# Signs written straight into the convolution's lanes, and another order of loads and stores

## What is computed

```python
x = channel_shuffle(x, 2);  xa, xb = split(x, 2, axis=1)
x1 = leaky_relu(gconv3x3(sign(x), w1, groups=2))        # 3x3, 64 -> 32 channels, 2 groups
x2 = batchnorm_train(x1, g1, b1)                        # statistics over all images
x3 = batchnorm_train(concatenate((x2 + xa, xb)), g2, b2)
x3 = channel_shuffle(x3, 2)
x4 = leaky_relu(gconv3x3(sign(x3), w2, groups=2))
x4 = batchnorm_train(x4, g3, b3)
out = concatenate((x4 + x3[:, :32], x3[:, 32:]))
```

## Time and profile before

| | us |
|---|---|
| median of 3 runs | 3279.19 (3274.48 to 3287.09) |
| profiled execution, device time | 3276.55 |
| its span, first to last instruction | 3274.8 |
| PE, PEld, DVE, ACT, POOL busy | 85%, 70%, 65%, 62%, 58% |
| mean granted TensorE clock | 0.943 of full speed |

### The profile page before, as it was taken

How to read it: one execution, slowest core, us unless ns; L and a number is a source line. 1 busy time by engine, 2 the same in 40 slices (tenths; PEclk the granted TensorE clock), 3 DMA queues, 4 the chain that set the end, 5 groups by cost and what they waited for, 6 DMA issues and landing times. The chain is left out here.

```text
span 3274.8 us, 116147 instructions
## 1 busy us (share of the span) xinstructions
PE 2788.1 (85%) x47624; PEld 2283.9 (70%) x47624; DVE 2114.6 (65%) x3114; ACT 2026.7 (62%) x4321; POOL 1900.8 (58%) x1450
## 2 busy tenths in 40 slices
PE   3888837777629999999989999999999999999992
PEld 2555525565428887888878778887888878878882
DVE  3445422222359878797887968778797877969660
ACT  1222112222248887888877877887888877878860
POOL 0000000000148888888887888888888888878870
PEclk9999968888869999999999999999999999999996
DMA  4555368888436766666666666666676666666552
GB/s 105 148 145 143 99 158 208 201 217 209 119 126 189 204 194 194 197 198 191 204 193 189 202 187 188 199 196 201 187 202 193 202 194 184 199 192 194 172 169 69
DMA packets 476972, 586.45 MB, mean 179 GB/s; under 512 B 175768, under 2 KB 420960, under 8 KB 476512
## 3 DMA queue, kind: packets, MB, share of 16 engines
q1 hardware_dynamic: 358240, 488.14, 54.1%
q10 hardware_dynamic: 118272, 91.76, 8.8%
HBM read 351.92 MB, written 201.14 MB: 169 GB/s over the span
## 5 line engine op out<-in xcount | busy, mean ns | idle before, releaser
L1251 PE MATMUL acc_p<-abuf,vbd 128*32 128x102 f32 (+7 forms) x27648 | 1088.2, 333 | 113.8 <-DMA abuf<-weight_scratch 110.4
L1251 PEld LDWEIGHTS acc_p<-abuf,vbd 128*32 128x32 f32 (+1 forms) x27648 | 907.1, 144 | 295.8 <-DMA abuf<-weight_scratch 128.0
L1088 ACT ACTIVATE dwt<-xp,wts 128x224 f32<-128x224 f32 x2016 | 799.7, 482 | 107.0 <-ACT wst L1111 101.7
L164 PE MATMUL cv<-cin,wb 128*64 128x392 bf16 x6912 | 636.3, 348 | 150.1 <-DMA cin<-sg 150.1
L960 DVE TENSOR_TENSOR pr<-mh_p,ht 128x864 f32<-128x864 f32 x672 | 668.9, 1051 | 23.2
L164 PEld LDWEIGHTS cv<-cin,wb 128*64 128x64 bf16 x6912 | 449.7, 115 | 330.6 <-issue 98.9
L1230 PE MATMUL win_p<-pr,smat 128*128 128x160 f32 x4032 | 610.4, 306 | 10.4 <-POOL pr L1046 8.5
L1230 PEld LDWEIGHTS win_p<-pr,smat 128*128 128x128 f32 x4032 | 555.9, 190 | 30.9 <-POOL pr L1046 8.9
L1029 POOL TENSOR_TENSOR dwt<-dwt 128x896 f32<-128x896 f32 x224 | 512.0, 2286 | 4.7 <-ACT dwt L1088 4.7
L1043 POOL TENSOR_TENSOR pr<-pr 128x576 f32<-128x576 f32 x224 | 317.1, 1416 | 283.3 <-DVE pr L960 283.3
L1172 PE MATMUL om_p<-wts,omin 64*64 64x216 f32 x3584 | 378.6, 351 | 2.4 <-issue 2.4
(11 more groups left out here) (137 smaller groups left out, 2820.2 us busy)
## 6 DMA issues: line engine op xcount, KB each, us to landing
abuf<-weight_scratch SPq DMA_DIRECT2D x1568, 120.0 KB, 2.6
weight_scratch<-wst ACTq DMA_DIRECT2D x224, 400.0 KB, 3.6
xt<-x SPq DMA_DIRECT2D x128, 392.0 KB, 8.5
rows_scratch<-vsb SPq DMA_DIRECT2D x224, 128.0 KB, 3.2
vbd<-rows_scratch SPq DMA_DIRECT2D x896, 32.0 KB, 2.8
cin<-sg SPq DMA_DIRECT2D x128, 203.0 KB, 3.5
x_scratch<-xt SPq DMA_DIRECT2D x64, 392.0 KB, 5.4
y<-x SPq DMA_DIRECT2D x64, 392.0 KB, 4.0
```

Of the source, the lines that this page charges most:

```text
L164: mm = pe.matmul(cv[c][64 * h:64 * h + 64, 0:CN], wb[:, layer, j, k, :], cin[:, u, r:r + CR, k % 3:k % 3 + W], start=(k == 0 and j == 0), ...
L1088: ins = act.activation(dwt[:, j % 2, k, :].rearrange("p (r w) -> p r w", w=W), image[:, r:r + BR, k % 3:k % 3 + W], ACT.Identity, scale=dw ...
L1251: mm = pe.matmul(acc_p[32 * (2 * s + b):32 * (2 * s + b) + 32, 0:TN].rearrange("p (k w) -> p k w", w=W)[:, k0:k1 + 1, x0:x1], vbd[0:K, 1 - ...
```

## The change

ScalarE signs 64 lanes at a time and writes them at once into `cin`, in the lanes that the convolution reads: four instructions of 64x1568 for two of 128x1568. `sg`, `move_signs` and the semaphores `signs_in`, `signs2` are gone; TensorE waits for the signs' own semaphore. The border columns are zeroed in `cin`.

In the first block SP issues x of pairs 0 and 1 right behind the first layer's weights; the second layer's weights are loaded and split in the next block, behind VectorE's statistics of pair 0. At the end of the first pass SP also issues `lin` of pairs 0 and 1 and x of pairs 1 and 0 for the second pass. In the second pass's loop the loads of `lin` (p + 2) and x (p + 3) stand ahead of the stores of x3 (p + 1) and of the result (p). VectorE gets a wait for x of its own.

```diff
-        sg = sb("sg", [128, 2, 2, HH, PW], bf16)
...
-        def move_signs(eng, u, done):
-            for t in range(2):
-                for h in range(2):
-                    eng.dma_start(cin[64 * t:64 * t + 64, u, 1 + HH * h:1 + HH * (h + 1), :],
-                                  sg[64 * h:64 * h + 64, u, t, :, :]).then_inc(done, 16)
+        def write_signs(act, p, u, t, bias):
+            for h in range(2):
+                lanes = slice(64 * h, 64 * h + 64)
+                a = act.activation(cin[64 * t:64 * t + 64, u, 1 + HH * h:1 + HH * (h + 1), 1:1 + W],
+                                   rows(xt[lanes, buf(p), t, :].rearrange("p a f -> p (a f)")),
+                                   ACT.Sign, bias=gs[lanes, u, 3, t:t + 1] if bias else 0.0)
+            return a
+        def split_weights(dve, layer, loads, start):
+            then = steps(dve, w_split, start)
+            dve.wait_ge(w_in, 16 * loads)
+            then(dve.tensor_copy(wb[:, layer, 0], wf[:, :, :]))
...
                         sp.dma_start(wf[at:at + CO, :, oc:oc + 16], w1t[:, :, 16 * t:16 * t + 16]).then_inc(w_in, 16)
+                load_x(sp, 0, x_in[0])
+                load_x(sp, 1, x_in[1])
+                sp.wait_ge(par_in, 32)
...
                 channel_stats(0, 0, 0)
                 group_stats(0, 0)
+                dve.memset(wf[:, :, :], 0.0).then_inc(w_zero, 1)
+                split_weights(dve, 1, 12, 5)
...
-                step(pairs - 4, 0, False)
+                step(pairs - 4, 0)
                 sp.wait_ge(used_ok, pairs - 3)
                 load_x(sp, pairs - 1, x_in[1])
-                step(pairs - 3, 1, False)
-                step(pairs - 2, 0, False)
-                step(pairs - 1, 1, True)
+                for u in range(2):
+                    sp.wait_ge(l1_out[u], 16)
+                    sp.dma_start(lin[:, u, :], l1_d[u, :, :]).then_inc(l1_in[u], 16)
+                step(pairs - 3, 1)
+                sp.wait_ge(used_ok, pairs - 2)
+                load_x(sp, 1, x_in2[1])
+                step(pairs - 2, 0)
+                step(pairs - 1, 1)
+                sp.wait_ge(used_ok, pairs)
+                load_x(sp, 0, x_in2[0])
...
                 def step(p, i, u, last):
-                    pe.wait_ge(signs_in[u], NS * i + NS)
+                    pe.wait_ge(sign_ok, p + 1)
...
                 with sp.Fori(0, pairs // 2 - 2) as i:
                     for u in range(2):
-                        step(2 * i + u, u, False)
                         load_l1(2 * i + u + 2, u)
                         settle(sp)
                         sp.wait_ge(x3_out[u], NX * i + NX)
                         load_x(sp, 2 * i + u + 3, x_in2[1 - u])
+                        step(2 * i + u, u, False)
...
+                    dve.wait_ge(x_in2[u], NX * i + NX)
```

More of the change, by code:

```diff
@@ L171, in evacuate, with steps @@
             act.activation(lt[:, u, CN * c:CN * (c + 1)], cv[c][:, 0:CN], ACT.Copy).then_inc(done, 1)
-        def steps(eng, done):
-            n = [0]
+        def steps(eng, done, start=0):
+            n = [start]
             def then(ins):
@@ L194, in _, with step @@
                         sp.dma_start(wf[at:at + CO, :, oc:oc + 16], w1t[:, :, 16 * t:16 * t + 16]).then_inc(w_in, 16)
+                load_x(sp, 0, x_in[0])
+                load_x(sp, 1, x_in[1])
+                sp.wait_ge(par_in, 32)
+            @block.gpsimd
+            def _(pool):
+                for col in (0, PW - 1):
+                    pool.memset(cin[:, :, 1:1 + H, col:col + 1], 0.0)
+                for row in (0, H + 1):
+                    pool.memset(cin[:, :, row, :], 0.0)
+                pool.memset(eps[:, :], EPS)
+                pool.memset(half[:, :], -0.5).then_inc(cleared, 1)
+                pool.wait_ge(cleared, 1)
+            @block.vector
+            def _(dve):
+                dve.memset(wf[:, :, :], 0.0).then_inc(w_zero, 1)
+                split_weights(dve, 0, 4, 0)
+        x_in2 = [sem("x_again0"), sem("x_again1")]
+        l1_in = [sem("l1_in0"), sem("l1_in1")]
+        l1_out = [sem("l1_out0"), sem("l1_out1")]
+        bx_ok, mv_ok, sq_ok, rhs_ok, grp_ok, neg_ok, m2_ok, var_ok, eps_ok, rstd_ok, sign_ok = map(sem, (
+            "bx_ok", "mv_ok", "sq_ok", "rhs_ok", "grp_ok", "neg_ok", "m2_ok", "var_ok", "eps_ok", "rstd_ok", "sign_ok"))
+        conv_ok, evac_ok, leaky_ok, cross_ok, used_ok = map(sem, ("conv_ok", "evac_ok", "leaky_ok", "cross_ok", "used_ok"))
+        with nc.Block() as block:
+            @block.sync
+            def _(sp):
+                def step(p, u):
+                    sp.wait_ge(leaky_ok, p + 1)
+                    sp.dma_start(l1_d[p, :, :], lt[:, u, :]).then_inc(l1_out[u], 16)
                 sp.wait_ge(w_zero, 2)
@@ L202, in _ @@
                                          w2t[t, :, :, 16 * q:16 * q + 16]).then_inc(w_in, 16)
[L203 to L225, removed]
@@ L228, in l0_passes @@
[L228 to L249, removed]
@@ L251, in _ @@
                 sp.wait_ge(x_in[0], NX)
                 load_x(sp, 2, x_in[0])
-                signs(0, 0)
                 with sp.Fori(0, pairs // 2 - 2) as i:
                     for u in range(2):
-                        step(2 * i + u, u, False)
+                        step(2 * i + u, u)
                         settle(sp)
@@ L524, in step @@
                                      lt[64 * h:64 * h + 64, u, :]).then_inc(l2_out[u], 16)
-                for p in range(2):
-                    load_x(sp, p, x_in2[p])
-                    load_l1(p, p)
                 sp.wait_ge(x_in2[0], NX)
                 load_x(sp, 2, x_in2[0])
-                x3_and_signs(0, 0)
+                store_x3(0, 0)
                 with sp.Fori(0, pairs // 2 - 2) as i:
                     for u in range(2):
-                        step(2 * i + u, u, False)
                         load_l1(2 * i + u + 2, u)
@@ L542, in _ @@
                 load_x(sp, pairs - 1, x_in2[1])
+                step(pairs - 4, 0, False)
+                load_l1(pairs - 1, 1)
                 step(pairs - 3, 1, False)
-                load_l1(pairs - 1, 1)
                 step(pairs - 2, 0, False)
```

29 lines of the change are left out of this document (12 added, 17 removed).

## The result

| | before | changed |
|---|---|---|
| median, us | 3282.87 (3274.48 to 3287.09, 4 runs) | 3111.57 (3106.56 to 3118.56, 4 runs) |
| profiled span, us | 3274.8 | 3109.1 |
| mean granted clock | 0.943 | 0.958 |

The ratio of changed to before is 0.9483, with a 95% interval of 0.9454 to 0.9511. The forecast was 3115, in a range of 3098 to 3160.

The account below looks back on a forecast made before the run. Bounds: SP's queue ring in the second pass, VectorE's ring in the first. Start -22.2, first pass 0, fold +2.7 and -24.2, second pass -118.3 sum to -162.0 us: from 3276.55 to about 3115, range 3098 to 3160.

Parts of the forecast that it names:

- the ring: Second pass, before: signs, copies, stores, load of `lin`, ScalarE, signs again; 26.90 us a pair against some 20 of TensorE.
- TensorE's 133 us: Second pass, before: TensorE idle 133.2 us ahead of the convolution, all put down to the DMA of the signs.

Follow-up runs that it names:

- the version with cross moments first: Changed kernel with first-pass VectorE reordered: leaky ReLU, cross moments, next-but-one pair's statistics, result's moments; x loaded ahead of the store; 3065.82 us.

## What to carry to other kernels

Look for the ring, not for the wait: TensorE's 133 us stood under the copies' name, and removing the copies alone made that pass 13 us slower. In a queue that one engine issues in order, put ahead of the stores the load that the next signs wait for; one DMA a pair was the whole gain of the order, and only then was the bandwidth of the copies worth having back. And once an engine is fed in one pass, ask what it waits for in the other: reordering VectorE's work took 51 us more off the first pass, the last 13 of them by moving four instructions of statistics into VectorE's idle time.

## What the runs showed of the hardware

The sign instruction on 64 partitions, with and without a bias. Two of every four write to other partitions than they read, and yet all of a form lie within 8 ns (source rows: min, median and max of one in ns):

```profile
L152 ACT ACTIVATE cin<-xt,gs x64: 1599/1602/1607, 20.7 to 355.0; 64x1568 bf16 x56, 64x1568 bf16<-64x1568 f32 x8
L152 ACT ACTIVATE cin<-xt x64: 1509/1512/1516, 408.4 to 684.4; 64x1568 bf16 x56, 64x1568 bf16<-64x1568 f32 x8
```

So a shift by 64 partitions costs nothing that shows, and half the partitions save nothing: on 128 the same signs took 1.60 us with a bias and 1.50 to 1.51 without (medians).

Stores of the kernel before ran at two rates with the DMA engines full both times: the store of all 128 partitions of `lt` to its own scratch, and the last store of the second pass, in two DMAs of 64 partitions to rows of twice that length (windows rows):

```profile
404.00:405.00 1.00, 0.00 (x0) 0.00 (x0) 1.00 (x3) 0.00 (x0) 0.00 (x0) 0.50 1.06 445
...
880.00:882.00 2.00, 0.00 (x0) 0.00 (x0) 0.93 (x2) 0.00 (x0) 0.00 (x0) 0.80 1.01 201
```

445 against 201 GB/s. Whether the number of partitions or the layout of the destination makes the difference was not tried.

A wait of 0.73 to 0.84 us in each of 14 pairs (the version with cross moments first) was never followed by a slow first chunk. Waits of 2.6 to 3.1 us were in 7 of 13 cases in the changed kernel's first pass, but waits of 2.3 to 2.8 us in only 3 of 15 in the second pass of the version with twice the signs.
